# Score products and row maxima of a batch one pass behind its split and loads, with a third set of score operands and values

## What is computed

```python
x = layernorm(x + attn0(x))   # 16 heads of 8 channels, scores - slope_h * |q - k|, softmax over all 256 keys
x = layernorm(x + ffn0(x))    # 8 experts, top 2 by softmax gate, silu(x w1) * (x w3) @ w2, plus one shared expert
x = layernorm(x + attn1(x))   # each query sees 44 fixed offsets back, softmax over them, sigmoid gate, w_out
x = layernorm(x + ffn1(x))    # 8 linear experts, top 2 by gate, softmax of the two logits
```

## Time and profile before

| what | value |
|---|---|
| median of 3 runs | 1671.92 us (1670.57 to 1673.61) |
| profiled execution | 1676.99 us, its span 1675.2 us |
| PE busy | 1446.3 us, 86% of the span |
| DVE busy | 1373.5 us, 82% |
| ACT busy | 914.0 us, 55% |
| POOL busy | 744.2 us, 44% |
| mean granted clock of TensorE | 0.956 of full speed |

### The profile page before, as it was taken

One profiled execution on the slowest core, in us unless ns is written; L12 is line 12 of the kernel. 1 busy time (PEld: TensorE's weight loads), 2 busy tenths in 40 slices (PEclk: granted clock), 3 DMA queues, 4 the chain that ended last, 5 costly groups with the idle time before them and its releaser, 6 DMA issues.

```text
span 1675.2 us, 34107 instructions
## 1 busy us (share of the span) xinstructions
PE 1446.3 (86%) x11872; PEld 1083.4 (65%) x11872; DVE 1373.5 (82%) x3772; ACT 914.0 (55%) x1836; POOL 744.2 (44%) x644
## 2 busy tenths in 40 slices
PE   2899899999999989999999999999999999997743
PEld 1477666666767666767676667676766676665532
DVE  2456888888898889888988888889888888887656
ACT  1356555666655656666555656665556566654410
POOL 0013555444455554434555544345555443455531
PEclk9799999999999999999999999999999999999755
DMA  3223344444442444434433444344334443433221
GB/s 99 100 74 99 114 112 126 130 113 112 110 111 93 113 130 130 126 99 105 116 99 107 130 130 130 96 109 113 101 107 127 130 130 96 109 110 87 75 50 33
DMA packets 83486, 179.29 MB, mean 107 GB/s; under 512 B 9746, under 2 KB 65810, under 8 KB 66194
## 3 DMA queue, kind: packets, MB, share of 16 engines
q1 hardware_dynamic: 83316, 177.12, 38.2%
...
## 4 chain that ended last, share of the span: by engine, by line
PE 53%; DVE 28%; issue 9%; ACT 4%; DMA 4%; SPq 1%; POOL 1%; DVEq 0%; ACTq 0%; POOLq 0%
PE bPV L519 7%; DVE mneg L1001 6%; PE bTU L466 5%; DVE nDy L941 5%; PE bS L536 5%; PE bTU L548 5%; PE bTU L549 4%; PE bPV L497 4%; DVE wb L964 4%; PE b L557 4%; PE bTU L481 4%; DMA wb<-d_w 2%; PE bS L539 2%; PE b L439 2%; ACT x L729 2%
## 5 line engine op out<-in xcount | busy, mean ns | idle before, releaser
L1001 DVE TENSOR_REDUCE mneg<-bS 128x2 bf16<-128x512 f32 x512 | 338.2, 687 | 53.2 <-PE bS L539 50.7
L1070 POOL TENSOR_TENSOR prod<-kC,qC 128x512 f32<-128x512 f32 x256 | 367.5, 1470 | 14.1 <-ACT kC L660 14.1
L1062 POOL TENSOR_TENSOR wb<-wb 128x1024 f32<-128x1024 f32 x64 | 150.7, 2355 | 458.8 <-DVE wb L903 458.8
L1082 POOL TENSOR_TENSOR h<-ub,gBcb 128x256 f32<-128x256 f32 x256 | 184.5, 729 | 300.1 <-DVE ub L1014 300.1
L688 ACT ACTIVATE P<-bTU 128x512 f32<-128x512 f32 x512 | 273.1, 599 | 19.7 <-PE bTU L483 19.2
L481 PE MATMUL bTU<-stack 97*128 97x256 bf16 x1024 | 220.6, 281 | 51.6 <-ACT P L688 51.5
L536 PE MATMUL bS<-stack 96*128 96x256 bf16 x1024 | 228.1, 283 | 36.7 <-DVE mneg L1001 14.5
L698 ACT ACTIVATE sil<-bTU,b 128x256 f32<-128x256 f32 x288 | 136.2, 474 | 220.2 <-PE bTU L549 129.0
L903 DVE TENSOR_TENSOR wb<-wb,vC 128x512 f32<-128x512 f32 x256 | 173.4, 728 | 76.5 <-DMA wb<-d_w 76.1
L548 PE MATMUL bTU<-x1T,w 128*128 128x256 f32 x576 | 184.9, 403 | 28.9 <-DVE nDy L941 28.7
L539 PE MATMUL bS<-dist,identh 128*128 128x128 f16 x1024 | 203.8, 225 | 0.0
...
## 6 DMA issues: line engine op xcount, KB each, us to landing
...
```

Of the source, the lines that this page charges most:

```text
L1001: v.tensor_reduce(mneg[:, :, k], bS[k % 2][:].rearrange("p (a b) -> p a b", a=TT), op=ALU.max, axis=AX.X, negate=True).then_inc(dveA1.done ...
L1070: tt_(prod[:, 2 * p:2 * p + 2, :], shifted(kC, p), qC[:].unsqueeze(1).to_broadcast([128, 2, T]), ALU.mult).then_inc(poolC1.done("prod", p), 1)
```

## The change

The score products by queries and their maxima become a stage of their own, S, with lag 1, and M moves with it to lag 1. Everything behind them (A2, A3, A3n, B, G, B2, C1, C2, C2n, D, D2) gets a lag that is larger by one. So the products of a batch no longer follow in the pass in which its parts are split, stored and loaded, but in the next, and the last lag is 7: there are 39 passes, and every stage is present in those from 7 to 31; pass 32 lacks A1 alone. Since a batch now needs its operands and values for one pass more, `stack` and `Vz` exist three times, by e modulo 3. In the setup this adds three loads and two memsets. The orders of all five engines are new.

```diff
-LAG = {"X": -1, "A1": 0, "M": 0, "A2": 1, "A3": 1, "A3n": 2, "B": 2, "B2": 3, "C1": 3, "C2": 4, "C2n": 5,
-       "D": 5, "D2": 6}
+LAG = {"X": -1, "A1": 0, "S": 1, "M": 1, "A2": 2, "A3": 2, "A3n": 3, "B": 3, "B2": 4, "C1": 4, "C2": 5, "C2n": 6,
+       "D": 6, "D2": 7}
...
     "pe": """
-        A1.qk B2.z A1.v A2.ST.0 A2.ST.1 A2.ST.2 A2.ST.3 A2.ST.4 A2.ST.5 A2.PV.0 A2.ST.6 A2.ST.7 B.xT A2.ST.8 A2.ST.9
...
+        B2.z A1.qk S.s.0 A1.v A2.ST.0 A2.ST.1 S.s.1 S.s.2 A2.ST.2 A2.ST.3 A2.ST.4 S.s.3 S.s.4 A2.ST.5 A2.ST.6
+        A2.PV.0 B.xT A2.ST.7 S.s.5 D.xT A2.ST.8 B.lg C1.xT D.lg S.s.6 A2.ST.9 A2.ST.10 A2.PV.1 A2.ST.11 C1.qk
...
     "sp": """
-        C2.wb A1.part.0 A1.part.1 A1.part.2 A1.rows.0 A1.rows.1 A1.rows.2 B.cT A3.x X.xT B.cb D2.out C1.dw M.m C1.wb""",
+        C2.wb A1.part.0 A1.part.1 X.xT A3.x A1.part.2 B.cT A1.rows.0 B.cb A1.rows.1 A1.rows.2 D2.out C1.dw M.m C1.wb""",
...
-        stack = [sb(f"stack{i}", [ROW_M + 1, 2, H, T], BF) for i in range(2)]
-
-        Vz = [sb(f"Vz{i}", [128, TT, H, 32]) for i in range(2)]
+        stack = [sb(f"stack{i}", [ROW_M + 1, 2, H, T], BF) for i in range(3)]
+
+        Vz = [sb(f"Vz{i}", [128, TT, H, 32]) for i in range(3)]
...
-                            sp.wait_ge(peA2.sem, peA2.count(e - 2, "ST", 15))
-                        sp.dma_start(stack[par][n:ROW_M:4, 1].rearrange("p h n -> p (h n)"),
+                            sp.wait_ge(peA2.sem, peA2.count(e - 3, "ST", 15))
+                        sp.dma_start(stack[e % 3][n:ROW_M:4, 1].rearrange("p h n -> p (h n)"),
...
-                        dve.wait_ge(pePV.sem, pePV.count(e - 2, "PV", 3))
-                        o = bass.AP(Vz[par], 0, [[TT * H * 32, 128], [64, TT * H // 2], [40, 2], [1, HD]])
+                        dve.wait_ge(pePV.sem, pePV.count(e - 3, "PV", 3))
+                        o = bass.AP(Vz[e % 3], 0, [[TT * H * 32, 128], [64, TT * H // 2], [40, 2], [1, HD]])
...
-                    if what == "A1.S" and (e := r["A1"]) is not None:
+                    if what == "S.s" and (e := r["S"]) is not None:
...
-                    if what == "A1.max" and (e := r["A1"]) is not None:
+                    if what == "S.max" and (e := r["S"]) is not None:
```

More of the change, by code:

```diff
@@ L56 @@
+        A2.PV.0 B.xT A2.ST.7 S.s.5 D.xT A2.ST.8 B.lg C1.xT D.lg S.s.6 A2.ST.9 A2.ST.10 A2.PV.1 A2.ST.11 C1.qk
+        A2.ST.12 A2.ST.13 S.s.7 S.s.8 A2.ST.14 A2.ST.15 D.y.0 C1.vg B.cT A2.PV.2 S.s.9 D.y.1 B.ab.0 A2.PV.3 B.ab.1
+        S.s.10 B.ab.2 S.s.11 D.y.2 A3.pT S.s.12 B.ab.3 B.ab.4 S.s.13 C2.out B.ab.5 S.s.14 C1.sc A3.aT C1.scT B.ab.6
+        B.ab.7 B.ab.8 S.s.15 B.z C1.wT A3.out D.y.3 M.mT""",
     "act": """
-        A1.qk A2.exp.0 A2.exp.1 A2.exp.2 A2.exp.3 A2.exp.4 A3n.nm B2.nm A2.exp.5 A2.exp.6 A2.exp.7 A2.exp.8 A2.exp.9
@@ L60 @@
     "dve": """
[L61 to L65, removed]
+        B2.res D2.mom N.root.0 S.max.0 A1.rest N.root.1 S.max.1 S.max.2 N.root.2 A1.v N.root.3 S.max.3 A1.mid A1.lo
@@ L66 @@
+        C2.pv.0 C2.pv.1 C2.pv.2 C2.pv.3 S.max.4 S.max.5 S.max.6 G.rank C2.pv.4 C2.pv.5 C2.pv.6 C2.pv.7 G.weigh
+        S.max.7 S.max.8 C2.add.0 D.acc.0 C2.add.1 D.acc.1 S.max.9 B.wu.0 B.wu.1 C2.add.2 S.max.10 C2.gt B.wu.2
+        D.acc.2 S.max.11 A3.rec S.max.12 C2.res A3.num S.max.13 B.wu.3 B.wu.4 B.wu.5 C1.mx S.max.14 S.max.15 B.wu.6
+        C1.sum B.wu.7 B.wu.8 A3.res D.acc.3""",
     "pool": """
-        C2.add.0 C2.add.1 C1.prod.0 C1.prod.1 C1.prod.2 C1.prod.3 C1.prod.4 C1.prod.5 C1.prod.6 C1.prod.7 C2.xb
@@ L227, in network @@
         actG = steps("actG", "ge")
-        dveA1 = steps("dveA1", "rest v mid lo max*16")
+        dveA1, dveS = steps("dveA1", "rest v mid lo"), steps("dveS", "max*16")
         dveA3 = steps("dveA3", "rec num*2 " + LN)
@@ L287, in passes @@
             for t in range(B + LAST):
-                one(t, t % 2, t)
+                one(t)
         block = ctx.enter_context(nc.Block())
@@ L301, in _ @@
                     sp.dma_start(dst[:, tt, :], bass.AP(A[name].tensor, 0, [[0, 128], [1, 128]])).then_inc(ld_const, 16)
-            for i in range(2):
+            for i in range(3):
                 for s in range(2):
@@ L307, in _, with one @@
                 sp.dma_start(dst[:], A[name]).then_inc(ld_score, 16)
-            def one(t, par, key):
+            def one(t):
                 r = stages(t)
                 for what, n in ORDER["sp"]:
-                    if key == 1 and (what, n) == ORDER["sp"][0]:
+                    if t == 1 and (what, n) == ORDER["sp"][0]:
                         for dst, name in expert_consts:
@@ L603, in one @@
                         take(7, ("M", actM, "mT", 0), t)
-                        pe.wait_ge(dveA1.sem, dveA1.count(e, "max", 15))
+                        pe.wait_ge(dveS.sem, dveS.count(e, "max", 15))
                         o = b7[:].bitcast(BF)
```

72 lines of the change are left out of this document (33 added, 39 removed).

## The result

| | before | after |
|---|---|---|
| median | 1672.76 us (1670.57 to 1674.89, 4 runs) | 1626.34 us (1622.32 to 1630.57, 4 runs) |
| ratio, 95% interval | | 0.9723 (0.9691 to 0.9754) |
| profiled execution, its span | 1676.99 us, 1675.2 us | 1623.99 us, 1622.2 us |
| fill, to the maxima's transpose (M.mT) of pass 5 before, pass 6 after | 251.4 us | 235.0 us |
| 26 passes, M.mT to M.mT | 1244.0 us | 1210.5 us |

The forecast was 1643 us, so the direction was right, and the fill was right to a microsecond. The full passes gave 21 us more than I had worked out. The two profiled executions lie 53 us apart and the medians 46: the one of before was 4 us slower than its median, the one of after 2 us faster.

A forecast was written before the change was run, and what follows sets the result against it. No single engine but a ring of dependences through PE and DVE bounds the pass. 1677 - 17 (fill) - 12 (full passes) = 1648 us profiled, 5 us less for the median: 1643 us; forecast 1625 to 1660, with rivals 1598 to 1690.

The forecast's parts named there:

- Fill: Opening passes: pass 2 no longer waits long for stack (13.8 us), the next four passes save 3.5 us; 17 us gained.
- The walk: Step-by-step timing of one full pass from B2.z: 47.0 us against 47.46, 12 us saved over 26 passes.
- Steps 1 to 3: Pass start to gates' last write: n_b ends 8.15 us, B.xT starts 10.3, max.6 14.15, gc ends 21.3.
- rival C: Row of maxima lands late for A2.ST.0; each 0.1 us beyond 3.3 costs 2.6 us; 1656 us with 0.5; 7%.
- Step 4: DVE's middle, from max.7 through C2's additions and C2.gt to max.11: 11.7 us, ending at 33.0.
- Step 5: PE's end, from S.13 to M.mT: 14.0 us, with 0.85 us waiting for ACT's copies ahead of C1.scT.
- rival F: Shorter, more frequent PE waits make the clock swing in full passes: 26 x 1.0 = 27 us, 1670 us; 4%.
- Drain: The stretch after the full passes: no change, plus or minus 5 us.
- B: Three maxima ahead of n_b delay the norms and each full pass by 1.5 us: 1694 us, slower; 17%.
- E: Pass 2 waits behind the weights, so no fill gain, but the steady gain comes: 1660 us; 5%.
- D: Only the fill gains; the full pass stays as long as it was: 1655 us; 13%.
- A: Spreading S fills both engines' gaps better than worked out: a pass of 45.2 us, 1595 us; 17%.

The follow-up runs named there:

- experiment 1: The changed code with lag and third buffers, but all five engine orders of the kernel before: 1672.01 us, ratio 0.9999.
- experiment 3: The changed kernel's lag, buffers and hand-spread score products and maxima, with the kernel before's orders for everything else: 1668.57 us, ratio 0.9976.
- Experiment 5: The changed kernel with n_b ahead of the first three maxima, PE's heads moved back, and A2.ST.2 written four times: 1625.12 us, ratio 0.9713.
- experiment 9: The changed kernel with expert 6 (B.ab.6) ahead of the transpose C1.scT on PE: 1604.92 us, ratio 0.9600.
- experiment 4: The changed kernel with n_b ahead of the first three maxima and PE's heads of S moved back to match: 1663.96 us, ratio 0.9953.
- experiments 1 to 3: The second: the kernel before (old lag), new orders for all but score products and maxima, placed late, and SP: 1771.67 us, ratio 1.0596.
- 8: The changed kernel with the gates weighed two C2.pv earlier on DVE, and G.ge earlier on ACT: 1644.12 us, ratio 0.9827.
- 7: The changed kernel with two sets of score operands (stack) instead of three: 1631.51 us, ratio 0.9749.

## Why the prediction was right, and where it was off

**Fill: right, in part by luck.** 17 us predicted, 16.4 measured. Its parts were off in opposite directions. Pass 2 starts at 51.25 us (51). Its first score product starts at 53.20 (53), but I had it wait for the loads until then, and it waits only for the projection ahead of it. Pass 3 was to start at 71.5 and starts at 73.9: I had summed the heads, A2.PV and small work to 18.5 us behind the first product, but PE is busy for 21.89 us in this pass. That is 11.4 us instead of 13.8. Passes 3 to 6 gave 4.5 us, not 3.5, and 0.5 us more to M.mT, since A1.qk now stands behind B2.z. What I had missed is that the lag is not enough for it: I put most of the fill's gain down to the lag, and experiment 1 has the lag and no gain. With S spread as well the gain is 4.8 us (experiment 3), and the trace points to the place of X.xT on SP for 4 us more; the rest comes with the orders of the other engines.

**Full passes: right direction, too small by 21 us.** Predicted -0.46 us a pass, 12 in all; measured -33.5. What was off:

- *The walk* gave 47.0 us and the pass is 46.33. Steps 1 to 3 hold to 0.2 us: n_b 8.15 and 8.16; B.xT 10.3 and 10.47; max.6 14.15 and 14.26; gc 21.3 and 21.4. The row of maxima lands in time, and A2.ST.0 starts at 748.11 without a gap, so rival C is out. Step 4 ends 0.4 us early, since I took C2.gt at its 1.24 us of before, and it takes 0.82 from start to start now. Step 5 was put at 14.0 us and takes 13.7, since C1.scT waits 0.59 us and not 0.85. Together 0.7 us, or 18 us over 26 passes. Against that, the usual pass of before is 47.42 us and not the 47.46 of the one pass I had read, which takes 1 us off.
- *The drops.* The walk gave the length of a pass at full clock, and I set it against one of before at full clock. The mean of before, 47.84, also holds 8 drops of 1.3 us, 10.4 us in all. After has two of 3.3 us, 6.6. That is 4 us in this pair of executions for which the sum had no term; rival F looked only at the other side.
- The rest, about 1 us, is pass 32, which lacks A1 and takes 45.5 us.

**Drain:** put at 0 and -3.1 us; inside its margin of 5.

**The rivals.** B, by the late norms, is out: n_b does end late, B.xT starts at 10.47 us instead of 8.8, and gc ends 1.6 us later. But PE and DVE did work meanwhile that they had done behind it, as the walk had it, and the pass got shorter. Experiment 5 doesn't bear on B, since there the maxima hold up B.xT as long as the norms had. E is refuted by pass 2, D by the passes. A had PE's and DVE's gaps vanish and the pass at 45.2; the change kept most of its gaps (3.4 us a pass on PE, 4.8 on DVE), but experiment 9 comes to 45.72 with a single step moved. F, the clock: the change has fewer drops than before, but experiment 4 shows how near it lay. By moving the roots ahead of three maxima, and PE's heads of S with them, every full pass gets one, and 31 us of the gain's 46 go in them. The Trainium skill ("TensorE: Matmul & The Clock Gate", "A second HAM failure mode") tells of another kernel in which short waits between groups of products make the clock swing. The rows of experiment 4 agree: PE idles for 1.56 of the 6.98 us ahead of the drop.

**What the change is, then.** Its gain is 16 us of fill, 28 us of shorter passes and 4 us of clock, with 3 us more in the drain. (These are sums of the profiled pair; pass 32 and some uneven passes make up the rest of its 53 us. Of the 46 us between the medians the shares are not known.) The shorter pass depends on the whole weave, as far as experiments 1 to 3 tried it. The ring of the changed kernel runs through both engines, with waits at B.xT for ACT's normalization (0.89 us), at max.6 (0.75), at S.13 (0.22) and at C1.scT (0.59). Closing the last gave 0.61 us (9), and making DVE's middle 0.65 us later cost 0.64 (8). The third stack has no part in it (7), and n_b 1.5 us earlier gave nothing, since the maxima took its place (5). Whether a shorter gc alone would pay was not tried free of the second wait for POOL. Which of the moved steps of the new orders gives which tenth of a microsecond of the 1.1 stays open.
